# A transformer block on one NeuronCore: a self group's transposes at the preceding round's end, and the second stack's values in a round's first step

## The reference, cut to what matters

```python
def _L0_xcond_ref(x, c, context, ...):
    c_proj = silu(c) @ W_mod + b_mod            # shift, scale and gate of attention and MLP
    x_norm = _ln(x) * (1 + scale_a) + shift_a
    q, k, v = split(x_norm @ W_qkv + b_qkv)     # 16 heads of 8 channels
    x = x + gate_a * (softmax(q k^T * hd**-0.5) v @ W_proj + b_proj)
    q_c = _ln(x) @ W_qc + b_qc
    k_c, v_c = split(_ln(context) @ W_kvc + b_kvc)
    x = x + (softmax(q_c k_c^T * hd**-0.5) v_c @ W_cproj + b_cproj)
    h = gelu((_ln(x) * (1 + scale_m) + shift_m) @ W_mlp1 + b_mlp1)
    return x + gate_m * (h @ W_mlp2 + b_mlp2)
```

## Time and profile before

| | us |
|---|---|
| median of 3 runs | 563.41 (561.05 to 566.6) |
| the profiled execution, own time | 562.12 |
| its span on the core | 560.3 |
| mean granted TensorE clock | 0.993 |

### The profile page before, as it was taken

How to read it: one execution, slowest core, us unless ns; L and a number is a source line. 1 busy time by engine, 2 the same in 40 slices (tenths; PEclk the granted TensorE clock), 3 DMA queues, 4 the chain that set the end, 5 groups by cost and what they waited for, 6 DMA issues and landing times.

```text
span 560.3 us, 16374 instructions
## 1 busy us (share of the span) xinstructions
PE 529.6 (95%) x6175; PEld 385.9 (69%) x6177; DVE 425.6 (76%) x1191; ACT 381.0 (68%) x889; POOL 276.7 (49%) x296
## 2 busy tenths in 40 slices
PE   7988999899999999999999999998999999999995
PEld 6745666566666666666667666665788888888885
DVE  4788889788989889788877567767586786786565
ACT  6547688578787787778777675555764864864862
POOL 5638759489497787888850412224124124124100
PEclk9999999899999999999999989999999999999999
DMA  4765645435144342343410010001011011010000
GB/s 133 161 175 137 180 129 155 103 98 135 37 128 121 98 132 81 107 120 97 108 52 6 2 30 27 1 19 39 7 42 50 26 38 51 25 39 12 20 20 19
DMA packets 52939, 41.47 MB, mean 74 GB/s; under 512 B 6369, under 2 KB 52226, under 8 KB 52866
## 3 DMA queue, kind: packets, MB, share of 16 engines
q1 hardware_dynamic: 50792, 36.72, 24.7%
q10 hardware_dynamic: 2074, 3.77, 2.4%
HBM read 12.16 MB, written 2.10 MB: 25 GB/s over the span
## 4 chain that ended last, share of the span: by engine, by line
PE 64%; DVE 14%; POOL 7%; DMA 4%; issue 4%; ACT 4%; SPq 3%; ACTq 0%; DVEq 0%; POOLq 0%
PE PS L959 31%; PE PS L1831 7%; PE PS L1797 6%; PE PS L1883 3%; DVE NM L1619 3%; PE PS L1895 3%; DMA Qs<-MT 3%; PE PS L995 2%; PE PS L1815 2%; PE PS L1853 2%; SPq L1346 2%; PE PS L1888 2%; DVE r_T L934 2%; PE PS L1763 1%; DVE r_R L937 1%
## 5 line engine op out<-in xcount | busy, mean ns | idle before, releaser
L1619 DVE TENSOR_REDUCE NM<-PS 128x4 f32<-128x512 f32 x256 | 163.5, 681 | 36.4 <-PE PS L1797 35.5
L1502 ACT ACTIVATE PR<-PS 128x512 f32<-128x512 f32 x256 | 139.7, 600 | 26.7 <-PE PS L1815 26.0
L1797 PEld LDWEIGHTS PS<-Ks,Qs 64*128 64x128 bf16 x1024 | 57.0, 94 | 52.4 <-DVE NM L1619 27.7
L1797 PE MATMUL PS<-Ks,Qs 64*128 64x128 bf16 x1024 | 83.0, 218 | 5.1 <-DVE NM L1619 3.4
L1815 PE MATMUL PS<-Qs,Ks 64*128 64x128 bf16 x1024 | 83.4, 218 | 4.3 <-DMA Qs<-MT 3.6
L1831 PE MATMUL PS<-PR,Va 128*32 128x128 f32 x2048 | 82.9, 280 | 0.0
L744 ACT ACTIVATE r_HID<-PS,ANC 128x128 f32<-128x128 f32 x224 | 62.5, 379 | 18.3 <-PE PS L959 18.3
L655 POOL TENSOR_TENSOR m_veps<-m_mv,m_eps 128x4 f32<-128x4 f32 x16 | 3.6, 228 | 130.9 <-DVE m_mv L821 130.9
L1815 PEld LDWEIGHTS PS<-Qs,Ks 64*128 64x128 bf16 x1024 | 56.9, 94 | 7.9 <-DMA Qs<-MT 4.2
L1831 PEld LDWEIGHTS PS<-PR,Va 128*32 128x32 f32 x2048 | 48.3, 109 | 20.1 <-ACT PR L1502 5.4
L959 PE MATMUL PS<-r_NXS,r_WNS 128*128 128x512 f32 x168 | 52.6, 421 | 0.0
(11 more groups left out here) (197 smaller groups left out, 1107.5 us busy)
## 6 DMA issues: line engine op xcount, KB each, us to landing
Qs<-Qp SPq DMA_DIRECT2D x96, 128.0 KB
Ks<-Kp SPq DMA_DIRECT2D x90, 128.0 KB
CTXG<-in_ctx SPq DMA_DIRECT2D x8, 256.0 KB, 3.7
r_CTX<-in_ctx SPq DMA_DIRECT2D x8, 256.0 KB, 2.9
r_CTXT<-in_ctxt SPq DMA_DIRECT2D x8, 256.0 KB, 3.2
out<-X SPq DMA_DIRECT2D x8, 256.0 KB, 2.3
X<-in_x SPq DMA_DIRECT2D x7, 256.0 KB, 4.5
W<-in_weights ACTq DMA_DIRECT2D x2, 855.0 KB
```

Source lines behind the costliest of these rows:

```text
L1502: nc.scalar.activation(PR[:, u, :], T_BANK[u % 2][:, :], ACT.Exp, scale=SCALE)\
L1619: nc.vector.tensor_reduce(out=NM[:, turn, at:at + 4, 0], in_=S_BANK[score_bank(c, u)[0]][:, :].rearrange("p (h k) -> p h k", k=P), axis=AX ...
L1797: last = nc.tensor.matmul(S_BANK[bank][:, j * P:(j + 1) * P], Qs[c.stack][rows, lo + j, cols], Ks[c.stack][rows, lo + j, cols], start=True ...
```

## The change

Three edits of the table of times, and a new division of one read.

- `xt_s` of a self group (groups 4 to 7) moves from 0.2 of round i to 30.0 of round i - 1, behind the preceding `yt_s`. ScalarE reads its first half at 30.1; VectorE reads the second half at 0.3 of round i, and waits for ScalarE's half by a new semaphore `xt_half`. ScalarE's read at 2.1 goes.
- `v1` moves from 8.0 (read 8.1) to 2.0 (read 2.1) in rounds 1 to 4.
- At the end of rounds 0 and 1 `proj_s` moves from 27 to 26 and `yt_s` from 30 to 29, where rounds 2 and later have them already.

```diff
@@ regular_steps
-            + fill_steps(0.2, "xt_s", i + 3, (0, 0.3), (1, 2.1))
+            + fill_steps(30.0, "xt_s", i + 4, (0, 30.1)) + [(0.3, "read", "xt_s", i + 3, 1)]
...
-            + fill_steps(8.0, "v1", i, (1, 8.1))
+            + fill_steps(2.0, "v1", i, (1, 2.1))
@@ round_steps, i == 0
-                  + fill_steps(27.0, "proj_s", 0, (0, 27.1), (1, 27.2)) + fill_steps(30.0, "yt_s", 0, (1, 30.1))
+                  + fill_steps(26.0, "proj_s", 0, (0, 26.1), (1, 26.2)) + fill_steps(29.0, "yt_s", 0, (1, 29.1))
+                  + fill_steps(30.0, "xt_s", 4, (0, 30.1))
@@ round_steps, i == 1
-            steps += (fill_steps(27.0, "proj_s", 2, (0, 27.1), (1, 27.2)) + fill_steps(30.0, "yt_s", 2, (1, 30.1))
+            steps += (fill_steps(26.0, "proj_s", 2, (0, 26.1), (1, 26.2)) + fill_steps(29.0, "yt_s", 2, (1, 29.1))
@@ build_block
+        xt_half = sem("xt_half")
...
+        def shared_turn(g):
+
+            return g < 2 or g > 3
@@ scalar body
-                    shared = isinstance(g, int) and g < 2
+                    shared = shared_turn(g)
...
-                        last.then_inc(setup_act, 1)
+                        last.then_inc(setup_act if g < 2 else xt_half, 1)
@@ vector body
-                elif ev[:2] == ("read", "xt_s") and ev[3] == 1 and isinstance(ev[2], int) and ev[2] < 2:
+                elif ev[:2] == ("read", "xt_s") and ev[3] == 1 and shared_turn(ev[2]):
...
-                    dve.wait_ge(setup_act, 3)
+                    if g < 2:
+                        dve.wait_ge(setup_act, 3)
+                    else:
+                        dve.wait_ge(xt_half, g - 3)
```

## The result

The changed kernel took 570.98 us (median of 4 runs, 567.81 to 574.43) against 562.23 us for the kernel before on the same chip (4 runs): ratio 1.0138, 95% interval 1.0089 to 1.0188. The profiled execution took 570.29 us with a span of 568.4. The two agree within their intervals; between them lies +1.2%, about 6.7 us. Forecast was +0.9%, 5.2 us.

What follows compares the result with a forecast made beforehand. It took TensorE (busy 95%) in lock step with the other engines as the bound; round losses of 4.5 us plus 0.7 for the moved `proj_s` gave 5.2, taking the median from 563.4 to 568.6 us, whole range 562.5 to 575.

Steps and rivals of the forecast that it cites:

- The stall: Before the `xt_s` transposes, behind step 28's value products: TensorE waits 1.05 us for VectorE to read `yt_s`.
- TensorE per start: At each round start TensorE is 1.65 us late at the q0 fill, 0.7 from step 8 on.
- `mv` late: VectorE's last statistics, where GpSimd's work starts, come 1.6 us late at each round start, bounds 0.7 and 1.9.
- the half on VectorE: VectorE's two operations reading half of `xt_s`, between maxima of steps 30 and 0, add an unhidden 0.68 us.
- What lateness costs by round: Later of TensorE's 0.7 and GpSimd's 1.6 less slack: rounds 1 to 4 lose 1.6, 0.7, 0.7, 1.5, sum 4.5 us.
- `proj_s`: Moving `proj_s` and `yt_s` earlier at the ends of rounds 0 and 1 costs 0.33 us each, 0.7 together.
- A: Rival, chance 0.10: the bank is free in time, TensorE saves 0.74 us at each round start, giving 561.1 us.
- B: Rival, chance 0.20: TensorE's lateness alone counts, 0.7 us at each round start, 3.5 in all, to 566.9 us.
- C: Rival, chance 0.10: GpSimd's lateness counts in every round, 1.6 us each start, 7.1 in all, to 570.5 us.
- D: Rival, chance 0.15: each of four new stalls brings half clock for 3 us, 6.0 us more, to 574.6 us.

Runs made afterwards that it cites:

- e12: The changed kernel run once more without any edit; ratio to the kernel before 1.0100.
- e3: The changed kernel, but in step 28 VectorE reads `yt_s` (writing `X`) before it divides the outputs; ratio to the kernel before 1.0072.
- e6: The kernel before with only `v1` moved, from 8.0 to 3.0, behind step 2's scores; ratio 1.0097.
- e1: The changed kernel with `v1` put back to 8.0; ratio to the kernel before 1.0129.
- e4: The changed kernel with both halves of `xt_s` read by ScalarE, at 30.1 and 0.3, none by VectorE; ratio to the kernel before 1.0124.
- e9: The changed kernel with the context's 256 KB load moved from 9.0 to 14.0; ratio to the kernel before 1.0105.
- e5: The kernel before with only `proj_s` at 26 and `yt_s` at 29 at the end of rounds 0 and 1; ratio 1.0020.
- e10: The kernel before with the context's 256 KB load moved from 9.0 to 14.0; ratio 0.9973.
- e7: The kernel before with the `ln_x` statistics moved from 2.2 and 3.2 to 5.2 and 7.2; ratio 1.0007.
- e8: The changed kernel with the `ln_x` statistics moved from 2.2 and 3.2 to 5.2 and 7.2; ratio to the kernel before 1.0066.
- e2: The kernel before with `xt_s` left at 0.2 and only its second half read by VectorE at 0.4 instead of ScalarE at 2.1; ratio 1.0061.
- e11: The changed kernel with `yt_s` read first in step 28, `xt_s` at 31.0 behind step 30's scores, VectorE's half at 1.3; ratio to the kernel before 1.0099.

## Why the prediction was right, and where it was not

The forecast of 568.6 us, +0.9%, lay 0.1 to 0.5 points low, and its mechanism is what the runs show: a full extra wait per start that nothing absorbs, and a late `mv` behind it.

- *The stall.* Forecast 1.05, measured 1.11 at every start of e12 and at three of the first profile, 0.86 at the fourth. e3 shows its price in the steps directly.
- *TensorE per start.* Forecast +0.7, measured +0.98. The q0 fill was 1.80 late for 1.65, step 6 gave back 1.00 as forecast (2.31 to 1.31), and step 8 took 0.18 more (2.29 to 2.47). That last bit stands in e6 too, with `v1` early, and not in e1, with `v1` at 8.0: it goes with the fill's new place (in e1 steps 0 and 2 take 0.15 more instead). This mis-sized term is 4 x 0.28 = 1.1 us.
- *`mv` late.* Forecast 1.6, measured 1.69, but for a partly wrong reason: "the half on VectorE ... nothing hides them". e4 takes the half away and `mv` doesn't move. Between `X` and `mv` VectorE waits for scores anyway; the late scores set `mv`, and the half fits in.
- *What lateness costs by round.* This is the step that failed. I took each round's slack from one profile: +0.9 beyond TensorE's part in round 1, 0 in rounds 2 and 3, +0.8 in round 4. The five profiles with the turn at 30 and a late `mv` (after, e1, e4, e9, e12) have mean landing parts of -0.04, 0.21, 0.95 and 0.68; the four with `mv` on time (before, e5, e6, e10) have 0.01, -0.15, 0.20 and 0.27. (e7 and e8 move the work ahead of the stack themselves and are left out.) e10's round 4 holds the wait for the context, not for a stack; without it the last of these means is -0.10 and not 0.27. The difference is then -0.05, 0.36, 0.75 and 0.78, in all 1.8. Taking in e2, e3 and e11 as well, whose `mv` is 1.0 to 1.6 late, it is -0.07, 0.49, 0.79 and 1.05, in all 2.3. Round 1 costs nothing more, rounds 3 and 4 cost most, and the sum is near the 1.7 of the forecast only because the errors cancel: that is luck. (The landing parts of single profiles sum up to anything from 0.4 to 3.3 with `mv` late, so these means hold to some half a us.)
- *Why so by round.* SP's list shows it. I took round 1 to have no slack because TensorE waits there; but SP waits 1.26 us for `MT` at step 10 of round 1 as it does in round 2, so the first stack is issued no later against TensorE's steps, and the DMA for step 22, issued later, landed sooner (3.8 to 4.7 us in e2 and the eight profiles with the turn moved, 4.3 to 5.2 in the other five; why, no run tells). In round 3 I saw no wait of TensorE and took that for slack; SP's list was full there, and the lateness went through to the last k0 issue. In round 2 the last issue hardly moves (5.8 to 6.3 us behind step 10's exponentials with the load in its old place), and what makes up the rest there stays open.
- *`proj_s`.* Forecast 0.7; the steps show 0.36 for round 0's end and 0.35 for round 1's, and by time it isn't seen (e5).

Together: 4 x 0.98 = 3.9, plus 0.7, plus 1.8 to 2.3, is 6.4 to 6.9 us, or ratio 1.011 to 1.012, between the two measured 1.0138 and 1.0100. In the same way (four start parts, the landing part of its own profile, 0.7 where `proj_s` is moved) e1 comes to 7.7 us (measured 7.3), e2 to 4.5 (3.4), e3 to 4.8 (4.0), e4 to 7.0 (7.0), e6 to 3.9 (5.5), e9 to 5.6 (5.9), e11 to 7.5 (5.6), all within their intervals, which are 3 to 9 us wide; e8 with 8.5 (3.7) and e10 with 1.6 (-1.5) are outside, so one profile's landing part doesn't always stand for the timed runs.

Of the rivals, A (a gain) is out: the bank isn't free in time. B, 3.5 us, lies below both intervals of the changed kernel or at their edge (from 5.0 and 3.4 us); with 0.98 for 0.7 it would be 4.6, which the times alone don't exclude. Against it stand the landing parts: 0.4 to 3.3, mean 2.2, in the eight profiles with a late `mv`, and -0.2 to 0.0 in before, e5 and e6. C, 7.1 us, is nearest in size to the measured 5.6 to 7.8, yet its reason (1.6 in every round) fails in round 1, and holds nearly in rounds 3 and 4. D is out: in all six profiles that have the turn at 30 and the stall of 1.1 us (after, e1, e4, e8, e9, e12), no stretch at half clock begins behind one of these stalls. The Trainium skill, "TensorE: Matmul & The Clock Gate", section "HAM oscillation — how this bites in real kernels", tells of a DMA wait in each pass, some 3 to 5 us long, that costs the full clock in each pass. It states nothing for stalls of 1.1 us, and the prediction took it further than it goes; at these stalls the traces show no drop.

Of the 8.2 us between the two first profiles, 2.2 lie ahead of the change's places: round 0 began 0.9 later, its first steps took 1.7 longer at half clock, and the next ones 0.4 less. Both vary between executions, as the next section shows.

## What to carry to other kernels

When a step that shares a buffer is moved earlier, follow the buffer both ways: who must have read it before, and which next user takes the wait if this one is spared it (e11). Compare the end of that reader with the end of the work just ahead of the new place; a difference of 1.05 us in the trace of before was the price of the stall to 0.06. An engine's stall in a lock-step loop also delays the side chains that start from the others, and how much slack those have can't be taken from the waits of TensorE in one profile. It wants several profiles, or a pair of experiments that delay one and not the other (e2 and e6), and a look into the side chain's own list: where SP waited 1.26 us for something else the lateness ended, where it waited 0.04 it went through.

## What the runs showed of the hardware

**The clock falls after some waits and not after others of the same length.** Windows of the changed kernel (busy us of PE, PEld, DVE, ACT, POOL, granted clock, DMA share, GB/s): two waits, each with the half-speed (1.2 GHz) stretch that came behind it.

```profile
35.56:37.35 1.79, 0.00 (x1) 0.00 (x0) 0.73 (x2) 0.52 (x2) 0.00 (x0) 1.00 1.14 299
37.34:44.17 6.83, 6.81 (x72) 4.32 (x76) 3.17 (x8) 4.30 (x10) 0.00 (x0) 0.50 0.09 23
102.25:103.86 1.61, 0.00 (x0) 0.00 (x0) 0.69 (x1) 0.09 (x1) 1.53 (x2) 1.00 1.06 217
105.61:109.02 3.41, 3.41 (x47) 2.05 (x47) 2.49 (x6) 1.62 (x4) 3.17 (x4) 0.50 0.52 137
```

In e4 the same place of round 1 shows a wait of 1.45 and full clock behind it, in e2 one of 1.22 and half clock:

```profile
102.40:103.90 1.50, 0.05 (x2) 0.01 (x1) 0.69 (x1) 0.14 (x1) 1.42 (x2) 1.00 1.12 208
104.00:108.00 4.00, 3.67 (x72) 2.17 (x69) 2.92 (x8) 3.01 (x7) 3.76 (x5) 1.00 0.84 185
```

```profile
99.20:100.40 1.20, 0.01 (x1) 0.00 (x0) 0.69 (x1) 0.10 (x1) 1.12 (x2) 1.00 1.11 202
102.48:105.90 3.42, 3.42 (x32) 1.57 (x34) 2.17 (x6) 1.21 (x3) 3.19 (x5) 0.50 0.53 142
```

So the length of the wait ahead doesn't decide it here. Before and e5 agree to 0.01 us in this wait, 1.42, and before ran at half clock from 101.9 to 105.3 while e5 kept the full clock. A half-speed stretch in round 0 makes step 2 longer by 0.9 to 1.7 us (3.10 to 3.84 for 2.17), and it comes and goes between profiles of kernels that are alike up to there.

**Round 0 starts late more often in kernels with the change.** The wait ahead of it, for a maxima DMA, was 1.79 to 2.06 us in six of the eight profiles with the turn moved, and at most 1.58 in the six others, though the order of work up to there is the same. With one profile each this may be chance; I did not try to settle it.
